# Routing per sequence inside the second attention, expert regions in DRAM, results scattered straight to the output

## The chip, the cores and the metric

The kernel runs on one core of one Trainium2 chip. A time is the device time of one execution in microseconds, first to last instruction with what lies around it, and the figure for a kernel is the median of its runs. The engines are TensorE (PE, with its weight loads as PEld), VectorE (DVE), ScalarE (ACT), GpSimd (POOL) and SyncE (SP); each works through its own list of instructions in order and waits on semaphores.

## What is computed

An input of 16 sequences of 256 tokens of width 192 goes through a token selection that keeps 179 tokens of each sequence, an attention with a tanh score, a quantised feed-forward, a second attention, and a mixture of 16 experts. Each of the last four adds to the residual `h`. What the change touches is the last of them and the place where it starts:

```python
h = h + _L1_attn_ref(_layernorm(h, axis=-1), ...)
t = _layernorm(h, axis=-1).reshape(-1, 192)      # 16 * 179 = 2864 tokens
idx = jnp.argmax(t @ Wg.T + bg, axis=-1)         # one of 16 experts for each token
for e in range(16):
    y = gelu(t @ W1[e].T + b1[e]) @ W2[e].T + b2[e]
    out = out + (idx == e)[:, None] * y
h = h + out
```

## The kernel before, in words

A sequence of 179 tokens lies in SBUF as two parts, 128 tokens and 51 (`TILES`), on partitions; `resid` holds the residual of all 16. The five stages follow one another. In the second attention every engine runs through one loop over `b`, written out 21 times (`B + 5`), in which each helper works on a sequence some steps behind `b`: scores, probabilities and projections of `b`, context and output projection of `b - 1`, layer norm and gate of `b - 3` and `b - 4`. The order of the helpers within one step is written by hand for each engine, and an engine that waits holds everything behind it in its list.

The helpers that matter here, by engine:

- PE: `score_round` (L1774, its matmuls at L1762), `gate_mm` (L1853), `context_first` and `context_last` (matmuls at L1808), `turn_peaks` (L1792, matmuls at L1796), `prob_round`, `qk_mm` (matmuls at L1733), `project1`, `v_mm`, and as the last thing of a step `gate_turn(b - 3)` (L1848, transposes at L1553), which turns the normed sequence for the gate.
- DVE: `max_round` (L1328, reduction at L1333), `gate_move` (L1397), `norm4` (L1383), `add_out1` (L1372) which adds the attention to the residual and takes the statistics of that sequence, `v_move`, and as the last thing of a step `xq_make` (its last instruction L1313).
- POOL: `pair_norms` (L663) once for two sequences: it waits for the statistics of both, then makes mean and reciprocal deviation in some twenty small operations, each waiting for the one before (first L675, last L696). In this loop POOL does nothing else.

After the loop the whole routing is done at once: DVE (L1448 to L1480) finds each token's expert and its slot in a list sorted by expert, PE helps with two prefix sums, POOL sends the normed rows to `xs_dram` with 24 indirect DMAs (L742), and after all of them have landed a loop over 38 tiles of 128 rows (`XT`) starts. For each tile SP loads the rows, PE turns them (L1919, L1920), multiplies with the expert's first matrix, turns and multiplies with the second; DVE copies that expert's first matrix to a fixed place (L1487), POOL the second (L752); ACT moves what PE made (the result at L952) and issues the store to `ys_dram`. After the last tile 24 indirect DMAs on POOL (L761) bring the rows back in token order, DVE adds them to the residual, and SP stores the result.

Of the kernel before, what the change touches and what calls it, by code (L numbers as in the profile page):

```python
# [5 lines left out]
F32 = mybir.dt.float32  # L6
BF16 = mybir.dt.bfloat16
# [11 lines left out]
TA = 128  # L19
# [33 lines left out]
SENDS = B + B // 2  # L53
# [3 lines left out]
def build(nc, I, out):  # L57
    ctx = ExitStack()
    with ctx:
# [23 lines left out]
        def carve(shape):  # L83
# [6 lines left out]
            if len(shape) == 2:  # L90
# [46 lines left out]
        w1q = sb("w1q", [128, 2, HID])  # L137
        w2f = sb("w2f", [128, HT, D])
# [18 lines left out]
              for n in range(2)]  # L157
        y_sb = sb("y_sb", [128, 2 * D])
# [14 lines left out]
        ctx1 = work[:, 2 * B * D:2 * B * D + ROUNDS * WIDE].rearrange("p (r t) -> p r t", t=WIDE)  # L173
        PT1 = ROUNDS * SLOTS1 * KEEP
        pt1 = [pt_region[:, n * PT1:(n + 1) * PT1].rearrange("p (r j t) -> p r j t", r=ROUNDS, j=SLOTS1) for n in range(2)]

        ew1 = [pt_region[:, 0:EXPERTS * D], pt_region[0:DB + 1, EXPERTS * D:2 * EXPERTS * D]]
        ew2 = [work[:, 2 * EXPERTS * D:3 * EXPERTS * D], work[0:DB + 1, 3 * EXPERTS * D:4 * EXPERTS * D]]
        xn4 = xn3
        KE = 2 * B * EXPERTS  # L180
        wg = sb("wg", [128, 2, EXPERTS])
        carved[0] = 0
        lower = carve([128, 128])
        ones = carve([128, 128])
        valid = sb("valid", [128, 2 * B])
        iota_e = sb("iota_e", [128, EXPERTS])
        iota_t = sb("iota_t", [128, XT])
        carry = carve([128, EXPERTS, 2 * B])

        gate = [pt_region[:, c:c + KE].rearrange("p (e k) -> p e k", e=EXPERTS)  # L190
                for c in (4 * PT_COLS, 2 * B * D, 2 * B * D + KE, 2 * B * D + 2 * KE)]
        xs = [pt_region[:, 2 * B * D + 3 * KE + n * D:2 * B * D + 3 * KE + (n + 1) * D] for n in range(4)]

        tile_w = [[[pt_region[0:rows, 2 * B * D + (4 * m + 2 * n + r) * D:2 * B * D + (4 * m + 2 * n + r + 1) * D]
                    for r, rows in enumerate((DA, DB + 1))] for n in range(2)] for m in range(2)]
# [5 lines left out]
        top = sb("top", [128, 2 * B])  # L201
# [3 lines left out]
        base = sb("base", [128, EXPERTS])  # L205
        ended = carve([128, XT, EXPERTS])
        owner = sb("owner", [128, XT])
        owner_i = sb("owner_i", [128, XT], I32)
        slot_f = sb("slot_f", [128, 2 * B])
        slot_i = sb("slot_i", [128, 2 * B], U32)  # L210
        odd_i = sb("odd_i", [128, B // 2], U32)
        joint_i = sb("joint_i", [128, B // 2], U32)
        zeros = sb("zeros", [128, D])
        exT = [[carve([DA, 128]), carve([DB + 1, 128])] for n in range(2)]
        eh = [carve([128, D]) for n in range(2)]
        ehT = [[carve([DA, 128]), carve([DB + 1, 128])] for n in range(2)]
        ey = [carve([128, D]) for n in range(4)]
        xs_dram = nc.dram_tensor("xs_dram", (XT * 128, D), F32, kind="Internal").ap()
        ys_dram = nc.dram_tensor("ys_dram", (XT * 128, D), F32, kind="Internal").ap()
# [138 lines left out]
        e_loaded = sem("e_loaded")  # L358
# [5 lines left out]
        g_step = sem("g_step")  # L364
        chosen = sem("chosen")
        prefix_psum = sem("prefix_psum")
        slots_ready = sem("slots_ready")
        sent = sem("sent")
        xs_loaded = [sem(f"xs_loaded{n}") for n in range(4)]
# [10 lines left out]
        ys_stored = [sem(f"ys_stored{n}") for n in range(4)]  # L380
# [6 lines left out]
        xq_step = sem("xq_step")  # L387
        small1 = sem("small1")
        back = [sem(f"back{n}") for n in range(4)]
        summed = sem("summed")  # L390
        joined = sem("joined")
        slots_joined = sem("slots_joined")
        parted = [sem(f"parted{n}") for n in range(2)]

        block = ctx.enter_context(nc.Block())


        def units(g):
            return min(UG, UNITS - g * UG)
# [1581 lines left out]
```

## Time and profile before

| | us |
|---|---|
| runs | 1564.34, 1564.94, 1581.31 |
| median | 1564.94 |
| profiled execution, its time | 1580.39 |
| profiled execution, its span | 1578.5 |
| busy: PE / DVE / ACT / POOL | 1161.5 / 1127.1 / 1003.3 / 868.2 |
| mean granted clock of TensorE | 0.912 of 2.4 GHz |

The span is from the first to the last instruction of the profiled execution. Busy times are sums over all stages; which engine sets the end changes from stage to stage, so they are read stage by stage. The stages of this execution: first attention to about 900, feed-forward to about 1020, second attention to about 1410, routing and sends to 1464, tiles to 1535, and the way back to 1578.5.

### The profile page before, as it was taken

How to read it: one execution, taken by the hardware profiler on the slowest of the kernel's cores; microseconds unless marked ns; L12 is line 12 of the kernel's file. 1: busy time of each engine (PE TensorE's matmuls, PEld its weight loads, DVE VectorE, ACT ScalarE, POOL GpSimd, SP SyncE). 2: the span in 40 equal slices, each digit the busy share in tenths (PEclk: the TensorE clock that was granted, in tenths of full speed). 3: DMA queues.
4: the chain of work that ended last, by engine and by line, in shares of the span. 5: the costliest groups of instructions: out<-in, count | busy, mean ns of one | idle time of the engine just before them, and what ended most of it. 6: DMA issues, size and time to landing. Idle time of an engine off the chain costs nothing.

```text
span 1578.5 us, 39532 instructions
## 1 busy us (share of the span) xinstructions
PE 1161.5 (74%) x16019; PEld 875.2 (55%) x16021; DVE 1127.1 (71%) x2120; ACT 1003.3 (64%) x977; POOL 868.2 (55%) x963
## 2 busy tenths in 40 slices
PE   0547778887778888778877598479999999850880
PEld 0335555665555656556655488356666666630880
DVE  6979899898889998898988658524666666532342
ACT  0129999999999999999999667322333333310440
POOL 3619788878888788888788824400111111116235
PEclk9889999999999999999999999757999999855895
DMA  7300000000000000000000000000000000051334
GB/s 200 103 0 2 2 2 2 2 2 2 2 2 2 2 2 2 2 2 2 2 2 2 1 1 0 1 0 1 2 3 2 3 3 2 2 123 54 97 95 120
DMA packets 39013, 33.65 MB, mean 21 GB/s; under 512 B 5411, under 2 KB 37352, under 8 KB 38856
## 3 DMA queue, kind: packets, MB, share of 16 engines
q1 hardware_dynamic: 28782, 22.44, 5.1%
q10 hardware_dynamic: 7516, 4.53, 1.0%
q0 software_dynamic: 2560, 4.41, 1.0%
q8 instruction: 121, 1.98, 0.5%
q14 instruction: 34, 0.28, 0.1%
HBM read 18.84 MB, written 11.89 MB: 19 GB/s over the span
## 4 chain that ended last, share of the span: by engine, by line
issue 30%; PE 23%; POOL 20%; ACT 13%; DVE 10%; DMA 2%; POOLq 1%; DVEq 1%; SPq 0%; ACTq 0%
POOL work L420 11%; ACT work L821 10%; PE psum L1593 8%; PE psum L1546 5%; PE psum L1547 5%; ACT pt_region L810 3%; DVE work L420 2%; POOL norm_wide L594 2%; PE psum L1620 2%; POOL xs_dram L742 1%; POOL work L761 1%; DVE work L1041 1%; PE psum L1606 1%; DMA work<-in_x 1%; POOL trstd L696 1%
## 5 line engine op out<-in xcount | busy, mean ns | idle before, releaser
L821 ACT ACTIVATE work<-work 128x2864 f32<-128x2864 f32 (+1 forms) x272 | 688.6, 2577 | 33.5 <-DVE work L420 32.8
L420 POOL TENSOR_TENSOR work<-shared 128x1253 f32<-128x1253 f32 (+1 forms) x272 | 611.9, 2261 | 133.3 <-PE psum L1593 125.7
L1593 PE MATMUL psum<-work,ws_place 128*32 128x179 f32 x8640 | 396.3, 325 | 167.6 <-ACT work L821 167.5
L420 DVE TENSOR_TENSOR work<-psum,shared 128x1611 f32<-128x1611 f32 (+3 forms) x288 | 486.5, 1722 | 0.6
L1593 PEld LDWEIGHTS psum<-work,ws_place 128*32 128x32 f32 x8640 | 261.3, 112 | 275.4 <-ACT work L821 216.2
L675 POOL TENSOR_TENSOR tsum<-tstats 128x4 f32<-128x4 f32 x16 | 3.6, 226 | 363.3 <-DVE tstats L1261 363.3
L1762 PE MATMUL psum<-shared 32*64 32x179 f32 (+1 forms) x1728 | 143.1, 369 | 8.2 <-DVE shared L1349 8.2
L1127 DVE SCALAR_TENSOR_TENSOR p_sb<-psum,bs_col,s_top 128x358 f32<-128x358 f32 x144 | 82.2, 571 | 43.9 <-PE psum L1606 30.7
L1762 PEld LDWEIGHTS psum<-shared 32*64 32x64 f32 (+1 forms) x1728 | 81.6, 160 | 57.0 <-issue 36.7
L1355 DVE TENSOR_SCALAR pt_region<-pt_region 128x1074 uint32<-128x1074 uint32 x48 | 34.6, 721 | 89.4 <-ACT pt_region L881 89.4
L810 ACT ACTIVATE pt_region<-psum,bs_neg 128x512 f32<-128x512 f32 x144 | 95.2, 662 | 1.6 <-PE psum L1606 1.5
L1606 PE MATMUL psum<-ident,p_sb 128*128 128x128 f32 x544 | 89.6, 286 | 0.4 <-ACT pt_region L810 0.4
L1333 DVE TENSOR_REDUCE peaks<-psum 128x6 f32<-128x1074 f32 x48 | 61.2, 1278 | 37.6 <-PE psum L1762 37.2
L881 ACT ACTIVATE pt_region<-psum 128x1074 int32<-128x1074 f32 x48 | 51.2, 1066 | 43.0 <-PE psum L1762 43.0
L1124 DVE TENSOR_REDUCE s_top<-psum 128x2 f32<-128x358 f32 x144 | 71.5, 496 | 6.0 <-PE psum L1593 6.0
L1606 PEld LDWEIGHTS psum<-ident,p_sb 128*128 128x128 f32 x544 | 60.1, 142 | 27.7 <-issue 23.0
L862 ACT ACTIVATE xqT<-psum 128x384 bf16<-128x384 bf16 x16 | 7.8, 490 | 100.2 <-PE psum L1726 100.2
L1534 PE MATMUL psum<-work,shared 128*128 (+1 forms) x128 | 33.1, 400 | 38.7 <-DVE shared L1054 38.5
L797 ACT ACTIVATE resid<-psum 128x192 f32 (+1 forms) x32 | 8.6, 321 | 72.5 <-PE psum L1534 72.5
L940 ACT ACTIVATE shared<-psum 128x128 f32<-128x128 f32 x38 | 10.5, 277 | 68.6 <-PE psum L1920 56.1
L1733 PE MATMUL psum<-xqT,w1p 128*128 128x179 bf16 x480 | 51.3, 261 | 1.8 <-ACT shared L872 1.0
L845 ACT ACTIVATE pt_region<-psum,b_col,w_scale 128x179 f32<-128x179 f32 x96 | 42.7, 497 | 15.5 <-PE psum L1547 15.4
(311 smaller groups left out, 2024.9 us busy)
## 6 DMA issues: line engine op xcount, KB each, us to landing
xs_dram<-zeros SPq DMA_DIRECT2D x1, 3648.0 KB, 13.3
pt_region<-xs_dram SPq DMA_DIRECT2D x38, 96.0 KB, 2.0
ys_dram<-shared ACTq DMA_DIRECT2D x38, 96.0 KB, 1.6
work<-in_x SPq DMA_DIRECT2D x4, 768.0 KB, 11.1
pt_region<-scores_dram SPq DMA_DIRECT2D x4, 512.0 KB, 5.7
pt_region<-in_L_ffn_W1T SPq DMA_DIRECT2D x1, 1536.0 KB
work<-in_L_ffn_W2T SPq DMA_DIRECT2D x1, 1536.0 KB
out<-resid SPq DMA_DIRECT2D x16, 96.0 KB
```

The lines of the kernel that those rows point to most:

```text
L420: ins = eng.tensor_tensor(dst[:, a * KEEP:e * KEEP].rearrange("p (u s) -> p u s", s=KEEP), k[:, h * KP:h * KP + KEEP].unsqueeze(1).to_broa ...
L810: act.activation(pt[b % 2][:, :, 256 * k:256 * k + 128 * w], bank_pt[p % 2].rearrange("p (s c) -> p s c", s=2)[:, :, 0:128 * w], ACT.Exp, ...
L821: act.activation(a, a, ACT.Tanh).then_inc(tanh_done, 1)
L1124: dve.tensor_reduce(top, s, AX.X, ALU.max).then_inc(top_step, 1)
L1127: dve.scalar_tensor_tensor(p_sb[p % 2][:, 0:w * KEEP].rearrange("p (a s) -> p a s", s=KEEP), s, bs_col[:, :], top.unsqueeze(2).to_broadcas ...
L1333: dve.tensor_reduce(peaks[:, r, :].rearrange("p (s k c) -> p k s c", s=2, k=4)[:, 0:3, :, HD], score_slots[r % 2], AX.X, ALU.max, negate=T ...
L1546: pe.matmul(out, lhs[0], rhs[0], start=True, stop=False)
L1547: return pe.matmul(out, lhs[1], rhs[1], start=False, stop=True)
L1593: ins = pe.matmul(bank_s[p % 2][32 * quad:32 * quad + 32, at:at + KEEP], ws_place[:, j, :], arg_slot(n)[:, u * KEEP:(u + 1) * KEEP], start ...
L1606: ins = pe.transpose(bank[:, 256 * s + 128 * a:256 * s + 128 * a + 128], src[:, a * KEEP + 128 * s:a * KEEP + 128 * s + 128], ident[:, :])
L1733: ins = pe.matmul(out, lhs, rhs, start=(n == 0), stop=(n == len(terms) - 1))
L1762: return pe.matmul(out, one[32 * j:32 * j + 32, r, lo:hi], two[32 * j:32 * j + 32, r, 0:KEEP], start=True, stop=True)
```

## The change

Routing moves into the loop over `b`. For each sequence DVE picks the experts (`choose`), PE makes the prefix sums one step later (`prefix_mm`), and DVE makes the slots (`place`), with a running count for each expert in `carry`. Each expert has a fixed region of `CAP` = 2944 rows in `xs_dram`, so that a slot is known at once. A row now has 386 columns (`RW`): the normed token, a one, the token's number, and its residual. Rows are put together in a ring of four buffers (`stage`): DVE writes the norm, ACT the residual (`stage_resid`), POOL the number (`stage_index`); `gate_turn` turns that buffer. POOL sends the rows of a sequence with two indirect DMAs (`send_rows`). The tile loop loads such rows, DVE adds the residual, and POOL scatters each tile straight to the output by the token's number; rows that hold no token carry a number beyond the output and are dropped. The pattern of such rows is written to all of `xs_dram` (49,024 rows of 1544 bytes) by 24 DMAs on SP near the start. The copy of the second matrix moves from POOL to ACT, in one instruction, and the weights of the experts are loaded earlier.

```diff
-SENDS = B + B // 2
+CAP = -(-B * KEEP // 128) * 128
+XS_ROWS = EXPERTS * CAP + (XT - CAP // 128) * 128
+RW = 2 * D + 2
+RING, TILE_RING = 4, 8
...
+            sp.wait_ge(pad_ready, 2)
+            for lo in range(0, XS_ROWS, 2048):
+                n = min(2048, XS_ROWS - lo) // 128
+                sp.dma_start(xs_dram[lo:lo + 128 * n, :].rearrange("(j p) d -> p j d", p=128),
+                             pad_row[:, :].unsqueeze(1).to_broadcast([128, n, RW])).then_inc(e_zeroed, 16)
...
+            sp.wait_ge(tiles_ready, 1)
+            for n in range(RING):
+                sp.wait_ge(sent[n], 32 * B // RING)
+            for i in range(XT):
+                row = sp.value_load(owner_i[i:i + 1, 1:2], min_val=0, max_val=XS_ROWS - 128)
...
+                sp.dma_start(xs[i % TILE_RING], xs_dram[bass.ds(row, 128), :]).then_inc(xs_loaded[i % TILE_RING], 16)
...
-            with pool.Fori(0, B // 2) as j:
-                pair_norms(j, 1)
...
+            def stage_index(c):
+
+                if c >= RING:
+                    pool.wait_ge(sent[c % RING], 32 * (c // RING))
+                pool.tensor_copy(stage[c % RING][:, :, D + 1].bitcast(I32), tok_idx[:, 2 * c:2 * c + 2]).then_inc(idx_ready, 1)
+
+            def send_rows(c):
...
+                pool.wait_ge(slots_ready, c + 1)
+                for t, rows in TILES:
+                    pool.indirect_dma_start(xs_dram[:, :],
+                                            bass.IndirectOffsetOnAxis(ap=slot_i[0:rows, 2 * c + t:2 * c + t + 1], axis=0),
+                                            stage[c % RING][0:rows, t, :], None).then_inc(sent[c % RING], 16)
+
+            for b in range(B + 6):
+                if b % 2 == 0 and real(b // 2 - 1, B // 2):
+                    pair_norms(b // 2 - 1, 1)
+                if real(b - 6):
+                    send_rows(b - 6)
+                if real(b - 3):
+                    stage_index(b - 3)
...
+            rows_out = out.rearrange("b k d -> (b k) d")
+            for i in range(XT):
+                pool.wait_ge(ey_ready, i + 1)
+                pool.indirect_dma_start(rows_out, bass.IndirectOffsetOnAxis(ap=xs[i % TILE_RING][:, D + 1:D + 2].bitcast(U32), axis=0),
+                                        ey[i % 4][:, :], None, bounds_check=B * KEEP - 1,
+                                        oob_is_err=False).then_inc(y_sent[i % TILE_RING], 16)
...
+            def stage_resid(c):
...
+                act.activation(stage[c % RING][:, :, D + 2:RW], resid[:, c + 1, :, :], ACT.Copy).then_inc(staged_in, 1)
...
+            def choose(b):
+
+                dve.wait_ge(gate_out, b + 1)
+                rlink(dve.tensor_reduce(top[:, :], logits[:, :, :], AX.X, ALU.max))
+                for t in range(2):
+                    ins = dve.scalar_tensor_tensor(best[:, t, :], logits[:, t, :], top[:, t:t + 1], iota_e[:, :], ALU.is_ge, ALU.mult)
+                rlink(ins)
+                rlink(dve.tensor_reduce(top[:, :], best[:, :, :], AX.X, ALU.min))
                 for t, rows in TILES:
+                    ins = dve.tensor_scalar(hot[b % 2][0:rows, t, :], iota_e[0:rows, :], top[0:rows, t:t + 1], None, ALU.is_equal)
+                ins.then_inc(hot_ready, 1)
+
+            def place(b):
+
+                dve.wait_ge(gate_out, b + 2)
+                rlink(dve.tensor_tensor(best[:, :, :], places[:, 0:2, :], carry[:, :].unsqueeze(1).to_broadcast(te), ALU.add))
+                dve.tensor_tensor(carry[:, :], carry[:, :], places[:, 2, :], ALU.add)
+                rlink(dve.tensor_tensor(best[:, :, :], best[:, :, :], hot[b % 2][:, :, :], ALU.mult))
+                rlink(dve.tensor_reduce(slot_f[:, :], best[:, :, :], AX.X, ALU.add))
+                dve.tensor_copy(slot_i[:, 2 * b:2 * b + 2], slot_f[:, :]).then_inc(slots_ready, 1)
...
                 if real(b + 2):
                     xq_make(b + 2)
...
+                if real(b - 5):
+                    place(b - 5)
+                if real(b - 4):
+                    choose(b - 4)
...
             def gate_turn(b):
                 pe.wait_ge(n4_ready, b + 1)
                 pe.wait_ge(added1, min(b + 3, B))
-                turn_wide(bank_pre, norm_wide).then_inc(gxT_psum, 1)
+                pe.wait_ge(idx_ready, b + 1)
+                pe.wait_ge(staged_in, b + 1)
+                turn_wide(bank_pre, stage[b % RING]).then_inc(gxT_psum, 1)
...
+            def prefix_mm(b):
+
+                pe.wait_ge(hot_ready, b + 1)
+                pe.wait_ge(gate_out, b + 1)
+                h, out = hot[b % 2], prefix_cols.rearrange("p (n e) -> p n e", n=3)
+                pe.matmul(out[:, 0, :], lower16[:, :], h[:, 0, :], start=True, stop=True)
...
                 if real(b - 4):
                     gate_mm(b - 4)
+                if real(b - 5):
+                    prefix_mm(b - 5)
```

The five matmuls of `prefix_mm` are in bf16, 16 columns each. The steps of the tile loop keep their order; its transposes are now 128 columns wide on both halves, and the loop is written out on every engine.

## Rows read from the trace of the kernel before

**Rows 1.** By stretch: length, PE, PEld, DVE, ACT, POOL busy, clock, DMA share, GB/s.
```profile
60.00:995.00 935.00, 721.57 (x11622) 542.30 (x11622) 810.07 (x1180) 826.97 (x565) 707.63 (x494) 0.97 0.01 2
...
1410.50:1431.00 20.50, 3.78 (x4) 1.17 (x4) 14.46 (x30) 0.00 (x0) 1.63 (x2) 0.58 0.10 21
1431.00:1464.30 33.30, 0.00 (x0) 0.00 (x0) 0.00 (x0) 0.00 (x0) 23.49 (x26) 0.50 0.23 71
1464.30:1534.00 69.70, 69.51 (x453) 66.58 (x453) 30.39 (x148) 37.41 (x151) 23.25 (x74) 0.95 0.34 99
```

**Rows 2.** Timeline around the end of one even step of the second attention.
```profile
1274.34 0.63 PE L1553 MATMUL psum<-ident,norm_wide 128*128 128x128 f32 x4
...
1274.92 0.20 POOL L675 TENSOR_TENSOR tsum<-tstats 128x4 f32<-128x4 f32 x1 [34.40 <-DVE tstats L1261]
...
1276.18 0.40 PE L1546 MATMUL psum<-wg,xT_wide 128*128 128x16 f32 x2
...
1276.91 0.22 DVE L1313 TENSOR_SCALAR xq<-work 128x128 bf16<-128x128 f32 x1
1277.16 1.28 DVE L1333 TENSOR_REDUCE peaks<-psum 128x6 f32<-128x1074 f32 x1
...
1277.18 0.51 PE L1808 MATMUL psum<-pt_region,shared 128*32 128x179 f32 x8
...
1281.26 0.20 POOL L696 TENSOR_TENSOR trstd<-trstd,tsum 128x4 f32<-128x4 f32 x1
```

**Rows 3.** The line of the indirect sends: durations, idle before them, time to landing.
```profile
L742 POOL DMA_INDIRECT xs_dram<-work,slot_i x16: 956/960/1306, 1429.1 to 1448.4; - x16
...
  issue: 7.0, 23
...
DMA to landing us min/median/max: 2.3/2.3/3.0
```

**Rows 4.** TensorE alone by stretch: busy time, then its clock.
```profile
1028.00:1088.50 60.50, 53.28 (x385) 0.50 0.00 1
1088.50:1092.00 3.50, 3.50 (x37) 0.96 0.00 0
1092.00:1366.00 274.00, 253.38 (x3221) 1.00 0.01 3
```

**Rows 5.** TensorE alone while POOL's last `pair_norms` runs.
```profile
1396.00:1399.00 3.00, 0.00 (x0) 0.50 1.09 348
```

**Rows 6.** Timeline: the same matmuls of four steps, b = 0, 1, 11 and 12.
```profile
1047.33 0.90 PE L1796 MATMUL psum<-ident,peaks 128*128 128x128 f32 x3 [1.81 <-DVE peaks_tail L1342]
...
1077.44 0.90 PE L1796 MATMUL psum<-ident,peaks 128*128 128x128 f32 x3 [0.34 <-DVE peaks_tail L1342]
...
1283.72 0.55 PE L1796 MATMUL psum<-ident,peaks 128*128 128x128 f32 x3 [1.00 <-DVE peaks_tail L1342]
...
1304.18 0.55 PE L1796 MATMUL psum<-ident,peaks 128*128 128x128 f32 x3 [1.00 <-DVE peaks_tail L1342]
```

**Rows 7.** Timeline: two small dependent operations of the routing on DVE.
```profile
1422.40 0.18 DVE L1463 TENSOR_SCALAR counts_i<-counts_i 128x16 int32<-128x16 int32 x1
1422.62 0.17 DVE L1464 CAST tiles_f<-counts_i 128x16 f32<-128x16 int32 x1
```

**Rows 8.** Timeline: end of the last `pair_norms`, first send, first tile, last result.
```profile
1399.74 0.20 POOL L696 TENSOR_TENSOR trstd<-trstd,tsum 128x4 f32<-128x4 f32 x1
...
1429.07 1.31 POOL L742 DMA_INDIRECT xs_dram<-work,slot_i  x1 [26.06 <-DVE slot_i L1480]
1429.46 0.26 DVE L1487 COPY pt_region<-pt_region 128x192 f32 x1 [0.71 <-issue]
...
1464.38 0.45 PE L1919 MATMUL psum<-ident,pt_region 128*128 128x128 f32 x1 [45.02 <-DMA pt_region<-xs_dram]
...
1534.91 0.33 ACT L952 ACTIVATE shared<-psum 128x192 f32<-128x192 f32 x1 [0.60 <-PE psum L1547]
```

**Rows 9.** The page's list of DMA issues: size and time to landing.
```profile
xs_dram<-zeros SPq DMA_DIRECT2D x1, 3648.0 KB, 13.3
```

More of the change, by code:

```diff
@@ L178, in build @@
-        ew2 = [work[:, 2 * EXPERTS * D:3 * EXPERTS * D], work[0:DB + 1, 3 * EXPERTS * D:4 * EXPERTS * D]]
-        xn4 = xn3
-        KE = 2 * B * EXPERTS
+        BLOCK = EXPERTS * D
+        ew1, ew2 = (work[:, 2 * n * BLOCK:2 * (n + 1) * BLOCK].rearrange("p (r c) -> p r c", r=2) for n in range(2))
+        FREE1 = 2 * PT1 + ROUNDS * WIDE
+        stage = [part.rearrange("p (t c) -> p t c", t=2) for part in
+                 (w1_store[:, 0:2 * RW], w1_store[:, 2 * RW:4 * RW], w2_store[:, 0:2 * RW], pt_region[:, FREE1:FREE1 + 2 * RW])]
@@ L181, in build @@
         wg = sb("wg", [128, 2, EXPERTS])
[L182 to L185, printed above, removed]
+        lower16 = sb("lower16", [128, 128], BF16)
+        ones16 = sb("ones16", [128, 128], BF16)
         iota_e = sb("iota_e", [128, EXPERTS])
[L187 to L191, printed above, removed]
@@ L388, in build @@
         small1 = sem("small1")
[L389 to L393, printed above, removed]
         block = ctx.enter_context(nc.Block())
@@ L649, in _ @@
             pool.memset(ctx1[:, :, :], 0.0)
+            pool.memset(ew2[:, 1, :], 0.0).then_inc(ew_blank, 1)
+            for n in range(2):
+                pool.memset(eh[n][:, :], 0.0)
             for n in range(2):
@@ L758, in _ @@
-            for m in range(B // 2):
-                need(pool, summed, 2 * m - 6)
-                for k, rows in ((4 * m, TA), (4 * m + 2, TA), (4 * m + 1, 2 * TB)):
-                    pool.indirect_dma_start(xn4[0:rows, k, :], None, ys_dram[:, :],
-                                            bass.IndirectOffsetOnAxis(ap=slots_of(k)[0:rows, :], axis=0)).then_inc(back[m % 4], 16)
+            pool.wait_ge(f_added, B)
+            for n in range(RING):
+                pool.memset(stage[n][:, :, D:D + 1], 1.0)
@@ L765, in _ @@
+            for n in range(TILE_RING):
+                pool.wait_ge(y_sent[n], 16 * len(range(n, XT, TILE_RING)))
         @block.scalar
@@ L1494, in expert_step @@
+            fetch(0)
+            for i in range(XT + 4):
                 if real(i - 2, XT):
                     dve.wait_ge(ehT_psum, i - 1)
-                    dve.tensor_copy(ehT[two][0][:, :], bank_pt[two][:, 0:128])
-                elif real(i, XT):
-                    need(dve, eh_psum, i)
+                    dve.tensor_copy(ehT[i % 2][:, :], bank_pt[i % 2][:, 0:WIDE]).then_inc(ehT_ready, 1)
                 if real(i + 1, XT):
-                    fetch(tile_w[0][1 - two], ew1, first).then_inc(w1_fetched, 1)
@@ L1502, in expert_step @@
[L1502 to L1517 removed]
+                    fetch(i + 1)
@@ L1942, in expert_step @@
                     need(pe, ey_ready, i - 4)
-                    product(out_banks[1 - two][:, 0:D], [x[:, :] for x in ehT[1 - two]], tile_w[1][1 - two]).then_inc(ey_psum, 1)
-            staged(pe, expert_step, (0, 8), XT, 4)
+                    product(out_banks[n][:, 0:D], halves(ehT[n]), [tile_w[1][n][:, r, :] for r in range(2)]).then_inc(ey_psum, 1)
 _TURNED = ["L0_attn_Wq", "L0_attn_Wk", "L0_attn_Wv", "L0_attn_Wo", "L0_ffn_W1", "L0_ffn_W2",
```

396 lines of the change are left out of this document (179 added, 217 removed).

## Prediction

> **What bounds the kernel now.** I read the busy times stretch by stretch first, then the timeline at the two places that the change touches, then the clock.
>
> In the second attention TensorE sets the pace: it is busy for 253.4 of 274.0 us in the steady part, at full clock [rows 4], and a step takes 20.46 us (1283.72 to 1304.18 [rows 6]). The other engines have gaps, but only in certain places. POOL is idle there except for `pair_norms`: it starts at 1274.92, when DVE has the second sequence's statistics, and ends at 1281.46 [rows 2]. PE's `gate_turn` of the same step starts at 1274.34, before that chain has even begun [rows 2]. That order is what the reader should keep in mind.
>
> Behind the loop the chip is nearly serial. From the end of the last `pair_norms`, 1399.94, to the first tile, 1464.38, pass 64.4 us [rows 8]: the last gates, 20 us in which DVE works alone on the routing, and 33 us in which only POOL works [rows 1]. The 38 tiles then run at TensorE's pace (69.5 of 69.7 us busy [rows 1]), some 1.83 us each. The last result is copied by 1535.24 [rows 8]; the span ends at 1578.5, so the way back costs 43.3 us.
>
> **What the change takes away.** *The way back.* Behind the last result stand now one addition, one scatter and its landing. The indirect sends land 2.3 to 3.0 us after issue [rows 3]; with a little around it 3.3 us stay, so 40.0 us go. Bounds: 36 to 41.
>
> *Routing and sends.* I count from the end of the last `pair_norms`. POOL then still issues two sends, each 0.96 us and 0.3 us of gap (7.0 us over 23 [rows 3]), 2.5 us, and the number of sequence 13: PE turns it at +2.9 instead of long before. Then sequences 13, 14, 15 go through turn, gate, prefix and place. DVE's `place` and `choose` are ten small operations at 0.22 us from start to start [rows 7], some 2.0 us; following turn, move, gate matmuls and DVE round for round at the lower clock I get 5 to 6 us for each of three rounds, plus the one-step lag of the prefix: the last slots are ready at +23.5. Two sends end at +26.1 and land at +28.4; a tile's load lands 2.3 later (the sends' landing as the nearest row): first tile at about +31. Gain 33.4 us; 25 to 38.
>
> *Tiles.* PE does nearly the same matmuls, so 1.83 us each stands. From the busy times divided by 38 [rows 1], ACT has 0.98 us per tile, loses a copy of 0.33 [rows 8] and gains the second matrix (POOL's 0.61), so 1.26; DVE has 0.80 and gains an addition of 0.33; POOL gets a scatter of 1.26 instead of copies. Register loads come on top. All lie below 1.83, not by much: I charge 4 us; -2 to +20.
>
> **What it adds to the loop.** *A wait of PE for POOL.* `gate_turn(b - 3)` now waits for `stage_index(b - 3)`. On POOL this stands, in every even step, behind `pair_norms(b // 2 - 1)`, which waits for the statistics of sequence `b - 1`, and these are made in the same step by `add_out1(b - 1)`, directly ahead of `gate_turn`. So PE waits for the whole chain and the two sends behind it. From the rows: the turn was to start at 1274.34, `pair_norms` ends at 1281.46 [rows 2], which is 7.1 us; a tiny copy of 0.2 us (like the small POOL operations) makes 7.35; two sends of 1.26 make 9.9. Behind PE's wait stands the next step's score round, for which DVE and ACT wait in turn; nothing hides it. It comes at b = 4 without sends (none is ready before b = 6), at b = 6, 8, 10, 12, 14 with them, and at b = 16, which is already in the count from the last `pair_norms`. Sum: 7.4 + 5 x 9.9 = 56.9 us. Odd steps have no `pair_norms`, and their sends are done early. This is read from the order of instructions and hardly uncertain: 45 to 65, the upper end if a send stretches as the first one did, 1.31 us beside DVE's copies [rows 3, 8].
>
> *The clock behind that wait.* In this trace TensorE idle behind POOL is at 0.50 of its clock, 1.2 of 2.4 GHz [rows 5]. And in this loop it is slow to come back: from 1028 to 1088.5 PE was busy for 53.3 of 60.5 us and stayed at the lower level, then it rose during a run of full-array matmuls in step 1 and stayed up until the loop's end [rows 4]. The step between the first two `turn_peaks` took 30.1 us, against 20.46 [rows 6], though it lacked context turn, projection and gate (the last with its turn 1.6 us at full clock [rows 2]). So half clock stretches the work by 1.6 or more; I take 1.75. After each of six stalls PE thus resumes slow. From the turn to `turn_peaks` are 9.4 us at full clock, 1274.34 to 1283.72 [rows 2, 6], so 16.4 slow. If the clock then rises where it did in step 1, 11.2 us behind `turn_peaks` (1077.44 to about 1088.6 [rows 4, 6]), those 11.2 stand for about 6.6: 11 us lost in all. Bounds: 0 if the clock doesn't fall, 6 if it comes back with the context matmuls early in the step, 15 for a whole step. I take 11: 66 us. The Trainium skill ("TensorE: Matmul & The Clock Gate", HAM oscillation) tells of a kernel that waited for DMA between bursts and began every burst at the low clock; by that rule each of the six bursts starts slow, and this trace agrees for the one idle stretch behind POOL [rows 5].
>
> *Prefix and DVE.* `prefix_mm` is five small matmuls; the gate's eight take 1.0 us, 1276.18 to 1277.18 [rows 2], so 0.5 us in each of 11 steps, 5.5 us. It also waits for `choose`, the last thing of DVE's step before. DVE ended `xq_make` at 1277.13, while PE went on with the contexts at 1277.18 [rows 2]: there is no slack, and 2.0 us more of DVE go on PE's path at the start of every even step; in the others the stall covers it. Five times 2.0: 10 us. Together 15.5; 6 to 25.
>
> *Hidden.* `stage_resid` is one ACT copy where ACT waits anyway. The norm loses two DVE copies. The pad writes are 75.7 MB; the zero write moved 3648 KB in 13.3 us [rows 9], so they take some 270 us from about 45 us on, when the DMA is 1% busy [rows 1] and the first to need them comes near 1000 us. Their cover is the first attention; what they might delay is code loading, a rival below.
>
> **Sum against the profiled execution:** 56.9 + 66 + 15.5 + 4 - 33.4 - 40.0 = +69. 1580.4 becomes 1649. That execution lies 15.5 us over the median, like one of the three runs (1581.3). One stay of the clock at its lower level more or less would make such a difference, which this trace alone can't show. On the median: 1564.9 + 69 = 1634.
>
> **Rivals.**
> - *The clock holds.* If 9.9 us of waiting don't bring the clock down or it comes back at once, only the stall is paid: 56.9 + 15.5 + 4 - 73.4 = +3, 1568. For it: PE's short waits in the steady part (20.6 of 274 us idle) never lowered it [rows 4]. Against it: rows 5. 12%.
> - *The clock never returns while the stalls last.* Both steps of a pair are slow, 15 us each: six times 30 instead of 11, +183, 1748. For it: the 60 us of rows 4. Against it: projection, values and gate follow one another at the end of each step, full-array work like that in which it rose. 6%; a mix with the likeliest lies between.
> - *Faster:* the stall is not there, that is, `pair_norms` is no longer ahead of the turn when it counts, because the even step's statistics reach POOL well before PE gets to `gate_turn`. Then the loop pays 15.5 and the tail gives 73.4: 1564.9 + 15.5 + 4 - 73.4 = 1511. Decides: statistics 7 us or more before the turn. In the rows they come 0.6 us behind its start, and PE and DVE wait for each other in the same order after the change. 8%.
> - *The scatter sets the tiles' pace.* Descriptors are made on POOL beside DVE's copies; the first send, beside them, took 1.31 instead of 0.96 [rows 3, 8]. Two such delays per tile would make 2.0 us with the gap, and waits on each other perhaps 2.5: 38 x 0.7 = +27 on the sum, 1661. 9%. The Trainium skill ("SBUF — State Buffer", SBUF: two separate sides) says that a DVE copy in a two-port mode keeps GpSimd from writing descriptors, and gives some 3.1 us for such a DMA instead of 0.62; by that figure, an estimate, the tiles would take 48 us more.
> - *Pad writes slow the first attention* by late code: ACT is busy for 827 of 935 us there [rows 1] and has no slack. 10 to 40 us more, 1659 in the middle. 8%.
>
> **How the numbers follow.** The likeliest case, 57%, gives 1634, by its own bounds 1590 to 1675. The range takes in the first, fourth and fifth rival and leaves out the faster one and the lasting low clock: 1560 to 1695. A measurement of this kernel can tell about 2% from no change, that is 1534 to 1596. Faster: 8% and a little of mixed terms, 0.09. Same: the 12% and the low edge of the likeliest, 0.15. Slower: 0.76.
>
> **What would show it.** In the new profile PE's L1553-like turn of the staged rows should stand idle for 7 us once and about 10 us in every second step, released by POOL; the clock in these steps at its lower level up to the projection; steps in pairs of about 30 and 33 us (stall included) rather than 20.5. The tile phase should begin some 30 us behind the last `pair_norms`, run at 1.8 to 2.0 us per tile, and end 4 us behind the last result. The prediction is wrong if PE's turn doesn't wait, if the clock stays at 1.0 in the loop, or if the first attention has become longer.

## The result, and the profile after

The changed kernel takes 1694.0 us (median; 1689.9 to 1696.6) where the kernel before took 1564.6 in the runs beside it: ratio 1.080, 95% interval 1.072 to 1.088. It is slower. The forecast was 1634, with a range from 1560 to 1695: the result lies inside it by 1 us. The profiled executions are 1580.4 before and 1696.6 after, 116.2 us apart, where the sum of the prediction was +69.

The two spans differ at four places, read from the timeline at the same landmarks as before:

| stretch | before | after | change | forecast |
|---|---|---|---|---|
| start to the end of the last `pair_norms` | 1399.9 | 1564.1 | +164.1 | +138.4 |
| from there to the first tile | 64.4 | 31.0 | -33.4 | -33.4 |
| first tile to the last result (before: copied; after: added) | 70.9 | 88.8 | +17.9 | +4 |
| last result to the end of the span | 43.3 | 10.9 | -32.4 | -40.0 |

First attention and feed-forward did not become longer: the first `turn_peaks` of the second attention starts at 1047.44, before at 1047.33 [rows 6], though the pad writes occupy the DMA at some 360 GB/s from about 50 to 260 us. (In the profiles of the experiments below, which leave these stages as they are, it starts at 1042.7 to 1049.2, so a difference of 0.1 us says no more than that the cost is within some 6 us.) What the second attention loses is more than the whole difference of the spans. The timeline of TensorE over one pair of steps, from the `turn_peaks` of b = 11 to that of b = 13 (start, duration, instruction; in brackets the idle time ahead of it and what ended it):

```profile
1384.36 0.90 PE L1802 MATMUL psum<-ident,peaks 128*128 128x128 f32 x3 [0.33 <-DVE peaks_tail L1355]
1405.13 0.18 PE L1874 MATMUL psum<-hot,lower 128*128 128x16 bf16 x1 [1.91 <-DVE hot L1442]
1414.84 0.91 PE L1802 MATMUL psum<-ident,peaks 128*128 128x128 f32 x3 [0.34 <-DVE peaks_tail L1355]
1440.39 1.09 PE L1559 MATMUL psum<-ident,w_store 128*128 128x128 f32 x4 [10.97 <-POOL w_store L742]
1445.45 0.17 PE L1874 MATMUL psum<-hot,lower 128*128 128x16 bf16 x1
1456.05 0.90 PE L1802 MATMUL psum<-ident,peaks 128*128 128x128 f32 x3 [0.34 <-DVE peaks_tail L1355]
```

From one `turn_peaks` (L1802) to the next pass 30.5 and 41.2 us, where each step took 20.46 [rows 6]. The large wait is the forecast one: `gate_turn` (L1559) stands for 10.97 us, released by POOL's copy of the token numbers (L742). The other, 1.91 us ahead of the first prefix matmul (L1874), is for DVE's `choose`. POOL's side of the same wait:

```profile
1429.98 0.20 POOL L703 TENSOR_TENSOR tsum<-tstats 128x4 f32<-128x4 f32 x1 [58.80 <-DVE tstats L1274]
...
1436.34 0.20 POOL L724 TENSOR_TENSOR trstd<-trstd,tsum 128x4 f32<-128x4 f32 x1
1437.51 1.04 POOL L751 DMA_INDIRECT xs_dram<-w_store,slot_i  x1 [0.98 <-POOL trstd L724]
1438.86 1.08 POOL L751 DMA_INDIRECT xs_dram<-w_store,slot_i  x1 [0.30 <-issue]
1439.94 0.19 POOL L742 COPY w_store<-tok_idx 128x2 int32<-128x2 int32 x1
```

The chain of `pair_norms` is 6.6 us long, then come 0.98 us of gap, two sends of 1.04 and 1.08 with 0.3 between them, and at last the copy of 0.19 on which PE waits. This answers to [rows 2], where PE's turn did not look at POOL at all.

The clock in stretches of that pair (length, PE, PEld, DVE, ACT, POOL busy, clock, DMA share, GB/s):

```profile
1386.00:1396.00 10.00, 9.62 (x70) 6.65 (x69) 2.73 (x5) 4.49 (x8) 0.00 (x0) 0.50 0.01 2
1396.00:1404.00 8.00, 7.22 (x77) 5.80 (x76) 4.87 (x18) 3.28 (x7) 0.00 (x0) 0.99 0.00 0
1404.00:1408.00 4.00, 2.87 (x48) 1.82 (x53) 2.45 (x9) 0.47 (x1) 0.00 (x0) 0.79 0.01 4
1408.00:1414.00 6.00, 6.00 (x51) 3.56 (x52) 2.21 (x2) 0.32 (x1) 0.00 (x0) 0.50 0.00 0
1414.00:1424.00 10.00, 9.29 (x66) 6.49 (x65) 3.67 (x12) 2.80 (x6) 0.00 (x0) 0.53 0.01 2
1424.00:1434.00 10.00, 5.43 (x59) 4.49 (x56) 6.45 (x24) 4.31 (x8) 3.13 (x17) 0.98 0.00 1
1434.00:1445.00 11.00, 4.61 (x28) 3.27 (x29) 1.37 (x3) 0.49 (x1) 6.40 (x16) 0.50 0.15 50
1445.00:1456.00 11.00, 10.71 (x98) 6.30 (x98) 3.35 (x8) 0.79 (x2) 0.00 (x0) 0.50 0.01 1
```

There are two falls in one pair. The clock, given as a share of 2.4 GHz (0.50 is 1.2 GHz), is back at 1.0 from 1396, falls right behind the wait for `choose` at 1405, is low up to about 1424, comes back, and falls again in the stall at 1430 to 1440. Before, TensorE was at 1.00 through all of this [rows 4]. The prediction had the second of these falls and not the first.

In the tile phase the chain that ended last no longer runs through PE alone; its longest pieces are now DMA transfers (start, duration, piece):

```profile
1653.90 3.23 DMA out<-shared,pt_region
1657.29 2.39 DMA pt_region<-xs_dram
1663.26 2.61 DMA out<-shared,pt_region
1666.03 2.48 DMA pt_region<-xs_dram
```

A scatter's landing releases a row buffer, the next load goes into it, PE waits for the load. And the end, where POOL works off a backlog of scatters behind DVE's last addition (1683.47):

```profile
1683.47 0.35 DVE L1522 TENSOR_TENSOR shared<-pt_region,psum 128x192 f32<-128x192 f32 x1 [0.32 <-PE psum L1553]
1683.59 0.98 POOL L769 DMA_INDIRECT out<-shared,pt_region  x1 [0.30 <-issue]
1684.88 0.99 POOL L769 DMA_INDIRECT out<-shared,pt_region  x1 [0.30 <-issue]
1686.17 0.98 POOL L769 DMA_INDIRECT out<-shared,pt_region  x1 [0.30 <-issue]
```

### The profile page after: what moved, and what is told of

Read it like the earlier page. It is cut to its first block, busy times and chain, and to the rows that moved or that the text cites. A ratio compares the mean times of both kernels' runs of the same rounds, so it can differ in the third digit from the quotient of the medians.

```text
span 1694.7 us, 39242 instructions
## 1 busy us (share of the span) xinstructions
PE 1265.2 (75%) x16097; PEld 935.0 (55%) x16097; DVE 1139.9 (67%) x2178; ACT 1019.3 (60%) x955; POOL 874.9 (52%) x934
## 3 DMA queue, kind: packets, MB, share of 16 engines
HBM read 20.42 MB, written 83.87 MB: 62 GB/s over the span
## 4 chain that ended last, share of the span: by engine, by line
PE 42%; POOL 17%; ACT 13%; DVE 12%; issue 10%; DMA 4%; DVEq 1%; SPq 1%; POOLq 0%; ACTq 0%
PE psum L1768 10%; POOL work L430 10%; ACT work L832 10%; PE psum L1599 8%; PE psum L1552 5%; PE psum L1553 4%; PE psum L1739 4%; PE psum L1814 3%; ACT pt_region L821 2%; POOL norm_wide L618 2%; PE psum L1626 2%; PE psum L1559 2%; DMA out<-shared,pt_region 1%; DMA pt_region<-xs_dram 1%; PE psum L1612 1%
## 5 line engine op out<-in xcount | busy, mean ns | idle before, releaser
L1768 PE MATMUL psum<-shared 32*64 32x179 f32 (+1 forms) x1728 | 187.8, 462 | 7.1 <-DVE shared L1362 7.1
L1768 PEld LDWEIGHTS psum<-shared 32*64 32x64 f32 (+1 forms) x1728 | 103.5, 203 | 78.8 <-issue 56.1
L920 ACT ACTIVATE xT_wide<-psum 128x384 f32<-128x384 f32 x16 | 7.8, 490 | 108.1 <-PE psum L1559 108.1
L769 POOL DMA_INDIRECT out<-shared,pt_region x38 | 37.4, 985 | 61.3 <-DVE shared L1522 56.0
L1739 PE MATMUL psum<-xqT,w1p 128*128 128x179 bf16 x480 | 60.7, 291 | 1.8 <-ACT shared L883 1.0
L899 ACT ACTIVATE pt_region<-psum 128x358 f32<-128x358 f32 x16 | 7.5, 469 | 90.5 <-PE psum L1814 90.5
```

Source lines behind the costliest of these rows:

```text
L1739: ins = pe.matmul(out, lhs, rhs, start=(n == 0), stop=(n == len(terms) - 1))
L1768: return pe.matmul(out, one[32 * j:32 * j + 32, r, lo:hi], two[32 * j:32 * j + 32, r, 0:KEEP], start=True, stop=True)
```

## The experiments

"Loop" is the time from `turn_peaks` of b = 3 to that of b = 15 in the profiled execution, twelve steps; before it is 245.6 us (1119.96 to 1365.58), after 407.7. Ratios are to the kernel before on the same chip, whose median was 1572.9 to 1578.3 in these sessions (1562.4 to 1583.2), 8 to 14 us over that beside the first result. Measured against a margin of 2%, e1 and e12 are open and e9 and e10 the same as before; the argument rests on how the experiments differ from one another, by the median and by the loop. Medians of different sessions are good to several us only.

| kernel | median us | ratio, 95% interval | loop us |
|---|---|---|---|
| changed | 1694.0 | 1.080, 1.072 to 1.088 | 407.7 |
| e1 token number first on POOL | 1607.9 | 1.022, 1.013 to 1.031 | 326.0 |
| e2 token number before the sends | 1659.0 | 1.051, 1.045 to 1.058 | 379.4 |
| e3 twelve row buffers | 1675.2 | 1.061, 1.054 to 1.069 | 407.6 |
| e4 before, with the stall | 1669.6 | 1.061, 1.054 to 1.068 | 343.8 |
| e5 = e1, `choose` earlier | 1529.2 | 0.972, 0.967 to 0.978 | 255.8 |
| e6 changed, `choose` earlier | 1634.1 | 1.041, 1.035 to 1.047 | 352.2 |
| e7 = e5 with twelve buffers | 1516.3 | 0.964, 0.959 to 0.969 | 252.7 |
| e8 changed, last waits on SyncE | 1692.9 (one run) | | |
| e9 = e1, `choose` before `place` | 1584.6 | 1.008, 1.003 to 1.012 | 312.6 |
| e10 = e1, wait for `choose` filled | 1582.3 | 1.004, 1.000 to 1.007 | 316.4 |
| e11 = e6, stall filled in part | 1633.6 | 1.034, 1.027 to 1.041 | 353.1 |
| e12 = e6, stall filled | 1623.6 | 1.026, 1.016 to 1.037 | 338.5 |

**e1, the stall taken away.** POOL's order in each step:

```
+                if real(b - 3):
+                    stage_index(b - 3)
+                if real(b - 6):
+                    send_rows(b - 6)
                 if b % 2 == 0 and real(b // 2 - 1, B // 2):
                     pair_norms(b // 2 - 1, 1)
-                if real(b - 6):
-                    send_rows(b - 6)
-                if real(b - 3):
-                    stage_index(b - 3)
```

> The changed kernel with one change of order on POOL: in each step the token-number copy comes first, then the sends, then the pair's norm chain, so that PE's turn no longer waits for that chain or for sends. Theory (the stall and the low clock behind it are the cost): the six waits of 8 to 11.7 us vanish and the clock holds; two steps take 43 to 46 us instead of 71.7, and the time falls by 5.5 x 27 = 148 us to about 1546. Rival (PE's second wait, some 1.9 us for choose at the start of every even step, or the prefix work by itself brings the clock down): only the waits go, two steps take about 60 us, and the time is about 1630. Rival (DVE has become the bound of the loop by its ten small operations): two steps take 50 us or more at full clock, about 1580.

Measured 1607.9: 86 us less than the changed kernel, where I expected 148. The stalls are gone, and PE now waits for `choose` in nearly every step (what TensorE waited for from 1114 to 1440: total, times, longest):

```profile
PE psum L1874 <- DVE hot L1442: 19.6, 11, 2.0
PE psum L1802 <- DVE peaks_tail L1355: 8.3, 13, 1.0
PE psum L1768 <- DVE shared L1362: 5.3, 12, 0.5
```

These waits are 20 us; the loop is still 80 us longer than before. The rest is the clock, which falls eight times in the twelve steps, seven times beside such a wait; around one of them (1260.69):

```profile
1256.00:1258.00 2.00, 2.00 (x26) 1.33 (x24) 1.92 (x7) 0.49 (x1) 1.28 (x8) 1.00 0.01 4
1258.00:1260.00 2.00, 0.66 (x6) 0.56 (x6) 1.83 (x11) 0.00 (x0) 1.53 (x9) 1.00 0.00 0
1260.00:1262.00 2.00, 1.31 (x21) 0.98 (x25) 1.90 (x6) 0.00 (x0) 1.45 (x8) 0.52 0.00 0
1262.00:1264.00 2.00, 2.00 (x30) 1.12 (x21) 0.15 (x2) 0.39 (x1) 0.94 (x6) 0.50 0.03 8
```

So the theory had only 86 of its 148 us, and the first rival named what was missing, if with too large a price (1630). There was a second cause that I had priced at its waiting time alone.

**e2, only the sends taken out of the stall.** The copy stands behind `pair_norms` and ahead of `send_rows`.

> The changed kernel with the token-number copy still behind the pair's norm chain on POOL, but ahead of the two sends. Theory (PE waits for what is queued ahead of the copy, each thing by its length): the wait in steps 6 to 14 falls from 11.0 to about 8.4 us, the clock still falls behind each, and the time falls by 5 x 2.6 = 13 us to about 1681. Rival (the length of the wait decides whether the clock falls, with 8 us short enough): another 11 us or more per pair go, 1620 or less.

1659.0, 35 us less. In steps 6 to 14 the waits fell from some 11 to 7.7 us, 17 us in the loop; the loop gained 28, so part of the gain is clock again. The forecast of 13 was too small, the rival's 74 much too large.

**e4, the stall alone, in the kernel before.**

```
                 pe.wait_ge(added1, min(b + 3, B))
+                pe.wait_ge(pair_norm, B + (b + 3) // 2 * 2 if b + 3 < B else 2 * B)
                 turn_wide(bank_pre, norm_wide).then_inc(gxT_psum, 1)
```

> The kernel before, with one wait added: PE's turn of the normed rows waits for the pair's norm chain on POOL, as it does in the changed kernel (no sends are ahead of it). Nothing of the routing is in the loop. Theory as predicted (a wait of 7.1 us, 11 us of clock behind it): seven pairs would lose 18 us less the parts outside the loop, 6 x 18 = 109, about 1674. Rival (the low clock lasts through the following step, stall or no stall, and the second fall in the changed kernel comes from this wait alone): 6 x 23 to 27, 1705 to 1725. Rival (the clock holds without the routing's work in the loop): 6 x 7.1 = 43, about 1608.

1669.6, at the theory's 1674. The waits are 51.5 us over 7, 7.4 each; the loop has six and is 98.2 us longer, so behind each 7.4 us stand 9.0 us of clock. The prediction's 11 was of the right order. The 9.0 is a mean of unlike courses: behind four of the six stalls (those that end at 1206, 1264, 1380 and 1438) the clock is back before `turn_peaks` and falls once more right behind the waits around it. Two steps take some 58 us here, against 71.7 in the changed kernel.

**e5 and e6, the wait for `choose` taken away,** without and with the stall. DVE's order in each step:

```
+                if real(b - 4):
+                    choose(b - 4)
                 if real(b):
                     power_round(b, 0)
+                if real(b - 5):
+                    place(b - 5)
+                if real(b):
                     power_round(b, 1)
                     power_round(b, 2)
...
-                if real(b - 5):
-                    place(b - 5)
-                if real(b - 4):
-                    choose(b - 4)
```

> The kernel of the experiment with the token number first on POOL, and in addition DVE does choose directly ahead of the first power round and place behind it, in the time in which it waits for ACT, instead of at the end of the step. Theory (PE's wait of 1.9 us for choose at the start of every step is what lowers the clock in 9 of 12 steps there): the waits go, the clock stays at 1.0, a step takes 21 us instead of 27.2, and the time falls by 12 x 6.2 = 75 us and a little at the loop's end, to 1525 to 1535. Rival (the prefix and gate matmuls, small as they are, lower the clock without a wait): the waits go, the clock falls as before, 1585 to 1595. Rival (DVE's total work bounds the step): steps of 24 us or more at full clock, about 1570.

> The changed kernel with the wait behind the pair's norm chain left in place, and only choose and place moved ahead in DVE's order. Theory (each wait lowers the clock on its own): the stall of 11 us stays, the low clock behind it lasts into the following step as in the kernel before with the added wait, the second fall goes, and two steps take 40.9 + 11 + 9.5 + 1 = 62.4 us instead of 71.7: 1694 - 5.5 x 9.3 = 1643. Rival (the stall alone keeps the clock low through both steps): 1685 to 1694.

Both medians came out as the theory had it: 1529.2 and 1634.1. Ahead of the power rounds DVE waits for ACT, and there the ten operations cost nothing. In e5 nine of the twelve steps take 20.54 us, so prefix and routing cost 0.1 us a step, and three, b = 3, 8 and 13, take 23.6. What TensorE still waited for from 1115 to 1371, and its clock in these steps:

```profile
PE psum L1803 <- DVE peaks_tail L1355: 12.0, 12, 1.0
PE psum L1769 <- DVE shared L1362: 6.1, 12, 0.5
```
```profile
1115.00:1371.00 256.00, 237.68 (x2923) 176.48 (x2923) 165.32 (x461) 100.03 (x192) 53.99 (x189) 0.96 0.06 18
```

The three long steps are not free of the clock: in each it falls right behind the two waits around `turn_peaks`, 1.00 and 0.51 us long, and is back some 7 us later. Here is step b = 8, whose `turn_peaks` starts at 1221.18:

```profile
1221.00:1223.00 2.00, 1.47 (x13) 1.27 (x13) 1.67 (x6) 0.32 (x1) 0.00 (x0) 1.00 0.00 0
1223.00:1225.00 2.00, 1.85 (x20) 1.06 (x21) 1.74 (x9) 0.41 (x3) 0.00 (x0) 0.74 0.04 8
1225.00:1231.00 6.00, 6.00 (x42) 4.53 (x40) 2.22 (x8) 3.49 (x6) 0.00 (x0) 0.52 0.00 1
```

In the other nine steps the same waits leave it at 1.00.

The changed kernel, e1, e6 and e5 form a square. Taking the stall away is worth 86 us with the wait for `choose` in place and 105 without it; taking that wait away is worth 60 us beside the stall and 79 alone. Together 165.

**e9, the wait for `choose` halved.** e1 with `choose` ahead of `place` at the same spot of DVE's order.

> The kernel with the token number first on POOL, where PE waits 1.95 us for choose at the start of each step and the clock falls in most of them. Only the order of DVE's last two jobs of a step is changed: choose first, then place, so that choose ends some 0.9 us earlier. Theory (it is the length of that wait that counts: PE has waits of 1.0 us ahead of turn_peaks in every step of the kernel before, and its clock holds): the wait falls to about 1.0 us, the clock holds in most steps, a step takes 21.5 us, and the time falls from 1608 to 1540 to 1550. Rival (any wait at this place, in front of the small gate and prefix matmuls, lowers the clock): steps of 26 us as before, 1595 to 1600. Between the two would mean that the clock falls in some of the steps.

1584.6, between the two and nearer to the rival. The waits are 1.1 us, and steps of 20 to 30 us follow one another without order. The clock falls ten times in the twelve steps, five times beside this wait and five times right behind the waits around `turn_peaks`, which are as long as in the kernel before. So neither side had it: a wait of 1.1 us at this spot lowers the clock in some steps, and in others the fall comes at the next waits.

**e10, the wait for `choose` filled with work.**

`filler` issues matmuls whose result nobody reads, here eight of 512 columns.

```
                 if real(b - 5):
+                    if real(b):
+                        filler(bank_s1, 8, 512)
                     prefix_mm(b - 5)
```

> The kernel with the token number first on POOL, where PE idles 1.95 us for choose in each step. PE now does eight 128x512 bf16 products, into a bank that is free and with a result that nobody reads, ahead of that wait: some 1.7 us at full clock, so that it arrives when choose is nearly done. DVE's work and order are unchanged. Theory (what lowers the clock is TensorE standing idle there, not DVE being late): the clock stays at 1.0 in nearly all steps, a step takes 20.5 + 2 = 22.5 us, and the time falls from 1608 to about 1550. Rival (the loop is paced by DVE's longer chain and the low clock is only its companion): 1600 or more.

1582.3, again between. Beside `choose` the clock now holds, as the theory had it. But in nine of the twelve steps it falls a little later, at the two waits around `turn_peaks`, which are as long as in the kernel before (1.00 [rows 6]):

```profile
1309.00:1310.00 1.00, 1.00 (x17) 0.72 (x8) 0.42 (x1) 0.00 (x0) 0.78 (x1) 1.00 0.49 184
1310.00:1311.00 1.00, 0.35 (x4) 0.11 (x1) 0.96 (x3) 0.00 (x0) 0.30 (x1) 1.00 0.12 24
1311.00:1312.00 1.00, 0.65 (x6) 0.65 (x7) 0.92 (x7) 0.00 (x0) 0.00 (x0) 1.00 0.18 51
1312.00:1313.00 1.00, 0.81 (x9) 0.61 (x8) 0.73 (x3) 0.15 (x1) 0.13 (x1) 1.00 0.05 19
1313.00:1314.00 1.00, 0.68 (x6) 0.51 (x6) 0.84 (x3) 0.51 (x2) 0.05 (x1) 0.65 0.03 8
```

**e11 and e12, the stall filled with work.** In e6, between the wait for `added1` and that for the token number, in even steps. e11 has 36 such matmuls in each; e12 has 36 in the first and 50 in the others. The edit of e11:

```
                 pe.wait_ge(added1, min(b + 3, B))
+                if b % 2 and b + 3 < B:
+                    filler(bank_pre, 36, 512)
                 pe.wait_ge(idx_ready, b + 1)
```

> The kernel with choose and place moved ahead on DVE and the stall of 11 us kept (1634 us). In the five even steps with a next one PE does 36 products of the same kind, 7.7 us at full clock, into its free bank between the two waits, and waits for POOL only after them. The stall's length is unchanged. Theory (of what the stall costs, 11 us per pair is waiting and 9.5 us is the clock behind it): the clock holds or comes back at once, and 5.5 x 9.5 = 50 us go, to about 1582. Rival (after the stall the loop needs a slow restart for other reasons, queues refilling): 1620 to 1634.

> The kernel with the stall filled by 36 products, which left PE a rest of 2.8 us without work in steps 6, 8, 10 and 12, and the clock fell in these; in step 4, where nothing was left, it held and the step took 28.4 us, 20.5 plus the stall of 8. Now 50 products stand in steps 6 to 14, 10.7 us, so that no wait is left; POOL's chain and sends are unchanged and PE reaches the turn as late as before. Theory (the clock behind the stall is a cost of its own, some 9.5 us per pair, and TensorE idle is its cause): two steps take 52 us instead of 61.4, and the time falls from 1634 by 5 x 9 = 45 us to about 1589. Rival (the clock falls at the next short wait instead, as with the filled wait for choose): 1615 to 1634.

e11 gave 1633.6, nothing gained: a rest of 2.8 us was left (3.3 in the first), and the clock fell in it or right behind it, as it had with 11. Where nothing was left (step 4, of 28.4 us) it held. e12 gave 1623.6, 10 us less than e6 (14 in the loop) where the theory wanted 45, and its rival is the one borne out: the clock stays at 1.0 through filler and turn, and falls at the waits around `turn_peaks` in six of the twelve steps (the profiled execution of e12, 1627.7, is the longest of its four).

```profile
1270.00:1275.00 5.00, 4.93 (x82) 3.00 (x71) 2.12 (x2) 0.79 (x2) 0.00 (x0) 1.00 0.04 12
1275.00:1280.00 5.00, 3.57 (x31) 2.33 (x32) 4.16 (x17) 0.66 (x2) 0.00 (x0) 0.82 0.01 3
1280.00:1285.00 5.00, 5.00 (x37) 3.67 (x37) 1.45 (x6) 2.93 (x4) 0.00 (x0) 0.50 0.00 0
```

**e3, the tile phase.** `TILE_RING` from 8 to 12, with semaphores of earlier stages used again for the four new buffers.

> The changed kernel with twelve row buffers in the tile phase instead of eight; nothing else is changed. Theory (a load waits for the landing of the scatter eight tiles back, and the chain scatter, landing, load, tile sets 2.3 us per tile): PE's waits for the row loads go, the 38 tiles take 70 to 75 us from the first tile to the last addition instead of 88.8, and the time is about 1679. Rival (descriptor writing on POOL beside DVE's copies sets the tiles' pace): still 88 us, 1694. Rival (the register loads ahead of the matrix copies of ACT and DVE set it): still 85 us or more.

1675.2, as the theory had it. PE no longer waits for rows behind the first two tiles; the 38 tiles take 75.3 us (1596.72 to 1671.99) instead of 88.8. Of the +17.9 thus 13.5 were the ring's and 4.4 are left. The scatter's pace was not the bound: its durations are 983/983/1012 ns (least, median, most) in the changed kernel beside DVE's copies and additions.

**e8, who waits at the end.**

> The changed kernel with the final waits for the scatters' landings taken from POOL and given to SyncE. In the changed kernel the last scatter lands at 1688.3 and the span ends 6.4 us later with no row on any engine. Theory (POOL's own end of program takes these 6.4 us, and begins only when its waits are over): the tail behind the last addition falls from 10.9 to about 8 us. Rival (the 6.4 us follow the last landing whoever waits): 10.9 us again.

Behind the last addition stand 9.3 us instead of 10.9, between the theory's 8 and the rival's 10.9; from the start of the last scatter to the end of the span pass 7.0 us instead of 8.5. So 1.5 us seem to belong to POOL's waits, and the larger part of the stretch without a row stays with either engine. It is one execution, and a scatter's landing varies by more than that, 2.1 to 3.4 us in this one; what fills the stretch stays open.

**e7, the three edits together.**

> The three edits together on the changed kernel: token number first on POOL, choose and place earlier on DVE, twelve row buffers. Theory (all three causes add): the time with the first two less 13.5 us, 1512 to 1522, 3% under the kernel before. Rival (a causes of the loop other than the two waits is left): over 1570.

1516.3, as the theory had it: 178 us under the changed kernel and 3.6% under the kernel before (0.959 to 0.969). Thus the change itself is a gain once PE waits for neither POOL nor `choose`. That this is near the 1511 of the prediction's faster rival is chance: the rival had no stall either, but kept the wait for `choose` at 10 us and knew nothing of its clock or of the ring.

## Why the prediction was near, and where it fell short

The direction and the larger cause were right. That 1694.0 still falls inside the range is luck: it is above 1675, the upper bound of the likeliest case, and the range went on to 1695 for late code and for a slow scatter, neither of which came. What filled that room was the clock behind the wait for `choose` and the ring of row buffers.

*The bound and the stall.* Right. PE's turn waits for the whole of `pair_norms` and the two sends, at b = 4, 6, ... 16 and in no odd step. Forecast 7.4 once and 9.9 five times, 56.9 us; measured 7.99, 11.45, 10.96, 10.96, 10.97 and 10.92, 63.3. The sum missed the gap of 0.98 ahead of the first send, and sends of 1.04 to 1.08 where I took the 0.96 of [rows 3].

*The clock behind the stall.* The mechanism was right, and the size somewhat too large: e4 has 9.0 us per stall, forecast 11, and e6, the changed kernel without the wait for `choose`, has 106.6 us more in the loop than before, of which 63 are stall and 1 prefix, so that 43 are left, 7 per stall. From the turn to `turn_peaks` at the lower clock pass 15.7 us (1440.39 to 1456.05), forecast 16.4. The prediction's own working, 7.0 us ahead of `turn_peaks` and 4.6 behind, makes 11.6, which it put down as 11. The Trainium skill ("TensorE: Matmul & The Clock Gate", HAM oscillation) describes a kernel whose every burst behind a wait starts at the low clock; by that rule each of the six bursts does, and this trace agrees: the clock is 0.50 in all six when the turn starts, as it is from 1434 to 1456 above. What "the clock holds" (1568) had for it, the short waits that never lowered it, was no evidence for a wait of 11 us.

*Prefix and DVE.* This is the step that failed. I took 2.0 us of waiting for `choose` in five even steps, 10 us, and that was right as a waiting time (1.9 us, five times, 9.6 us). I gave it no clock, because PE's short waits in the kernel before had never lowered it. It did: e6 shows that without this wait the changed kernel takes 60 us less, of which 10 are waiting and some 50 clock, and e1 against e5 gives 79 us, of which 20 are waiting. The five prefix matmuls, which I put at 5.5 us, cost about 1. To the last `pair_norms` the changed kernel lost 164.1 us: 63 of stall, 10 of waits for `choose`, 1 of prefix, and by difference 90 of clock, where the forecast had 66. The near total hides two errors: about half of the 90 belongs to the stalls (43 by e6, 54 by e4), for which I had 66, and the other half to the waits for `choose`, for which I had nothing. DVE's total work does not bound the step (e5).

*Start of routing and sends.* Forecast 33.4 us gained, first tile at +31; measured 33.4 and +31.0. That it fits so well is partly luck: the last slots were ready at +21.2 (forecast 23.5) and the last send ended at +24.4 (26.1), but the sends took a median of 3.4 us to land, where I took 2.3.

*Tiles.* Forecast +4, measured +17.9. The sum looked at each engine's work per tile, and there it holds: e3 has +4.4. It did not look at the length of the way that a row buffer takes, from load through four tiles of work, scatter and landing back to load, which is over eight tiles' time at PE's pace. The rival on the scatter had the place (27 us in its sum, 48 by the estimate beside it) but not the mechanism. The Trainium skill ("SBUF — State Buffer", SBUF: two separate sides) has descriptor writing kept waiting by DVE copies; with scatters of 983 to 1012 ns this trace doesn't show it.

*The way back.* Forecast 3.3 us behind the last result, measured 10.9: 2.35 us until the last of the scatters in the backlog starts, 2.1 to its landing, and 6.4 without a row, which the sum did not have.

*Pad writes.* Hidden, as forecast.

*The median.* 1694.0 lies 60 us over 1634. The four terms miss 25.7 + 0 + 13.9 + 7.6 = 47 us in the profiled executions; the other 13 are the profiled execution of before, 15.5 us over its median, where that of after is 2.6 over its own.

**What stays open.** Why the same waits around `turn_peaks` lower the clock in one step and not in another. Their length doesn't decide it, nor the spot, nor what stands ahead. In the loop of the kernel before it never falls at them. In e5 it falls in every fifth step, though in steps 4 to 8 TensorE has the same work and the same waits. And e11 and e12 run the same instructions up to step 5, with the same waits and with steps of 20.42 and 28.4 us ahead; in step 5 the clock then holds in e11 (first line) and falls in e12 (second):

```profile
1169.00:1175.00 6.00, 5.49 (x70) 4.15 (x69) 4.42 (x17) 3.35 (x6) 0.00 (x0) 1.00 0.00 0
1169.00:1175.00 6.00, 6.00 (x46) 3.85 (x46) 3.08 (x14) 2.15 (x5) 0.00 (x0) 0.50 0.00 0
```

So the place of the waits in time must matter besides; against what it counts no run here shows. This open point bounds what can be claimed for the stall: e12 recovers 14 us of the loop (e6 to e12) where e4 charges 54 to the clock. And it bounds what is claimed for the wait for `choose`: that removing it gives 60 to 79 us is measured, but the falls it causes come in part at the waits behind it.

## What to carry to other kernels

When an instruction gets a new wait, read in order what is queued ahead of its releaser on that engine, and put the small job first (here a copy of 0.2 us, with the sends behind it): that was worth 86 to 105 us, without any work removed. Where TensorE sets the pace at full clock, a new wait of 2 us per step must be priced with the clock and not by its length; here it cost 60 us in place of 10, and 79 in place of 20. Moving the cause of both waits out of the way gave nearly all of the loop back (255.8 us in e5 against 245.6); filling the wait with work gave 26 us (e10) and 10 us (e12). Of a ring of buffers count the whole way round, landing and load included, not the busiest engine's work per item.

## What the runs showed of the hardware

Behind waits of 1.0 and 0.5 us around `turn_peaks` the clock stayed at 2.4 GHz in all twelve steps of the kernel before; it fell to 1.2 GHz there in three of twelve in e5 and in nine of twelve in e10. With a wait of 1.9 to 2.0 us in nearly every step (e1) the mean clock of the loop was 0.77 of 2.4 GHz, without it (e5) 0.96. Work put in front of a wait that left a rest of 2.8 us of 11 gained nothing (e11).

In the lines below POOL's indirect scatter starts 0.8 us after the addition that it waited for has ended; where it has not to wait it starts 0.30 us behind the one ahead (lines of the first section):

```profile
1677.71 0.33 DVE L1522 TENSOR_TENSOR shared<-pt_region,psum 128x192 f32<-128x192 f32 x1
...
1678.85 0.98 POOL L769 DMA_INDIRECT out<-shared,pt_region  x1 [1.24 <-DVE shared L1522]
```

75.7 MB of pad writes, 24 transfers at some 360 GB/s, stood beside a first attention in which ACT is busy for 827 of 935 us [rows 1]; no delay of the next stages is seen beyond the 6 us by which executions differ.
